# Spreading the idle groups of an edge loop between its blocks, and moving one small subtraction from ScalarE to VectorE

## The reference, cut to what matters

```
Wh    = xn @ W_w + W_b
e     = leaky(Wh[dst] . a_dst + Wh[src] . a_src + a_b, 0.2)
m     = segment_max(e, src)
ex    = exp(e - m[src])
att   = ex / segment_sum(ex, src)[src]
h     = relu(segment_sum(att * Wh[dst], src))
x     = x + h + mix(xn)
x     = x + ffn(layernorm(x))
```

## Time and profile before

| | us |
|---|---|
| three runs | 2430.62, 2435.78, 2439.38; median 2435.78 |
| the profiled execution | 2439.61, its span 2437.9 |
| first gather to last group's sums (in the edge loop) | 754.87 to 1914.06 |
| busy in the span: PE, DVE, ACT, POOL | 1952.8, 1758.0, 1440.8, 1129.3 |

### The profile page before, as it was taken

The page is one execution under the profiler, slowest core; times in us unless marked ns, Lnnn a source line. Parts: engine busy times, 40 slices in busy tenths (PEclk is TensorE's granted clock), DMA queues, the critical chain, the costliest instruction groups (busy, mean ns, idle before and its releaser), DMA issues. The chain is left out here.

```text
span 2437.9 us, 50376 instructions
## 1 busy us (share of the span) xinstructions
PE 1952.8 (80%) x10273; PEld 1581.1 (65%) x10273; DVE 1758.0 (72%) x5447; ACT 1440.8 (59%) x4447; POOL 1129.3 (46%) x1089
## 2 busy tenths in 40 slices
PE   2888856598874888988889998998799564399997
PEld 1444435477762777767677877777678463288886
DVE  7877769999984778787768888887788752155543
ACT  3566547233311778877778888887688762133332
POOL 0000000011125777777777777777720177455555
PEclk9899967799986999999999999999999875699998
DMA  4200000011112444444444444444410455255553
GB/s 136 59 26 27 28 2 22 13 55 23 24 21 76 121 118 116 122 124 117 121 117 118 121 117 121 117 116 121 124 41 6 123 141 139 75 88 92 94 97 57
DMA packets 123284, 205.68 MB, mean 84 GB/s; under 512 B 34806, under 2 KB 77667, under 8 KB 122987
## 3 DMA queue, kind: packets, MB, share of 16 engines
q0 software_dynamic: 69648, 135.12, 23.8%
q1 hardware_dynamic: 48681, 59.88, 8.3%
q10 hardware_dynamic: 4658, 7.46, 1.1%
HBM read 146.67 MB, written 49.70 MB: 81 GB/s over the span
## 5 line engine op out<-in xcount | busy, mean ns | idle before, releaser
L1306 POOL DMA_INDIRECT area<-wh_table,area x812 | 783.8, 965 | 260.1 <-issue 246.4
L1619 PE MATMUL bank<-area 128*126 x2008 | 512.4, 399 | 103.8 <-ACT area L1542 70.1
L1619 PEld LDWEIGHTS bank<-area 128*126 128x126 f32 x2008 | 366.6, 192 | 186.8 <-issue 134.0
L1340 DVE TENSOR_SCALAR area<-iota_row,area 128x126 f32<-128x126 f32 x1004 | 357.9, 364 | 33.1 <-ACT area L1495 27.5
L1528 ACT ACTIVATE area<-iota_row,area 128x126 f32<-128x126 f32 x753 | 292.4, 389 | 0.4 <-ACT area L1535 0.3
L1409 DVE SCALAR_TENSOR_TENSOR acc_mem<-acc_mem,area,bank 125x258 f32 x251 | 120.7, 481 | 179.6 <-PE bank L1607 168.1
L1542 ACT ACTIVATE area<-area 128x126 f32<-128x126 f32 x753 | 243.1, 387 | 0.5
L2110 POOL DMA_INDIRECT out_dram<-area x108 | 169.2, 1567 | 158.7 <-DVE area L2171 142.3
L519 POOL IOTA acc_mem<- 50x812 f32 x1 | 0.8, 807 | 457.7 <-DVE area L789 457.7
L1481 ACT ACTIVATE area<-bank 125x512 bf16<-125x512 f32 x251 | 148.7, 592 | 95.8 <-DVE area L1350 94.0
L1639 PE MATMUL bank<-area 128*128 128x250 f32 x800 | 191.0, 382 | 4.0 <-ACT area L1555 4.0
(11 more groups left out here) (395 smaller groups left out, 4217.1 us busy)
## 6 DMA issues: line engine op xcount, KB each, us to landing
area<-moe_rows SPq DMA_DIRECT2D x54, 264.0 KB, 2.7
area<-wh_table,area POOLq DMA_INDIRECT x812
area<-area SPq DMA_DIRECT2D x18, 388.5 KB, 3.4
wh_table<-area SPq DMA_DIRECT2D x50, 126.5 KB
xn<-in_x_dram SPq DMA_DIRECT2D x25, 250.0 KB
x_rows<-area SPq DMA_DIRECT2D x25, 250.0 KB
area<-x_rows ACTq DMA_DIRECT2D x24, 250.0 KB
area<-in_L_ffn_expert_w_dram SPq DMA_DIRECT2D x3, 1536.0 KB, 12.1
```

What stands on the lines that cost most here:

```text
L1306: g.indirect_dma_start(out=gath[:, (i + GT) % RS, :], out_offset=None, in_=table, in_offset=bass.IndirectOffsetOnAxis(ap=idx_tab[:, i:i + ...
L1340: ins = V.tensor_scalar(xm[:, b, t, :], iota_row[:, :], rowl[:, j % 10, t:t + 1], fetched(j, D)[:, t:t + 1], ALU.is_equal, ALU.mult)
L1619: last = T.matmul(bank[US[b]][0:RW, 0:WROW], sm[:, b, t, :], gath[:, bass.ds(place + t, 1), 0:WROW].rearrange("p a w -> p (a w)"), start=( ...
```

## The change

1. **Table.** The groups that no edge needs (`left` of them) are dealt out between the blocks: behind block i−1 there stand `int(i * left / 50 + 0.25)` of them in all. They carry block number 50, a 51st block of `acc`, `own_all`, `fr_c`, `peak` and `iota_blk` that nothing reads, and the first tile of the block that comes next. The table is worked out with a few more DVE instructions; two more small matmuls turn `tf` into a column for the ring's counts.
2. **Maximum.** `own_second` leaves ACT; `row_second` does the same subtraction on DVE, two slots behind the group's number, between `mark(2)` and `score_edge`. `d_m` now counts four steps to a group, and `a_own` one.
3. **Clearing.** The part of `acc_mem` from `ZERO_FROM` on (7798 of 13158 columns lie before it) is cleared ahead of the wait for the edge table; the rest is cleared in the loop, by a stage `clear` that runs once, at the end of slot 3, and `gather_up` of group 0 waits for it.

```
-        acc_mem = sb("acc_mem", [128, NT * WROW])
+        acc_mem = sb("acc_mem", [128, (NT + 1) * WROW])
+        acc_all = acc_mem[0:R, :].rearrange("p (b w) -> p b w", w=WROW)
...
+                V.tensor_tensor(packed[:, 3, :], firstf[:, 1:NT + 1], firstf[:, 0:NT], ALU.subtract)
                 step(V.tensor_tensor_scan(gend, ones[:, 0:NT], ngf, 0.0, ALU.mult, ALU.add))
...
+                step(V.tensor_scalar(left, gend[:, NT - 1:NT], -1.0, float(NG), ALU.mult, ALU.add))
+                V.tensor_copy(packed[:, 4, :], firstf[:, 1:NT + 1])
+                step(V.tensor_scalar(lastf, iota_g[:, 1:NT + 1], left, 1.0 / NT, ALU.mult, ALU.mult))
+                step(V.tensor_scalar(int50, lastf, 0.25, None, ALU.add))
+                step(V.tensor_copy(sparef[:, 1:NT + 1], int50))
+                V.tensor_tensor(packed[:, 0, :], gend, sparef[:, 1:NT + 1], ALU.add)
+                step(V.tensor_tensor(ngf, ngf, sparef[:, 1:NT + 1], ALU.add))
+                V.tensor_tensor(packed[:, 1, :], gend, sparef[:, 0:NT], ALU.add)
+                step(V.tensor_tensor(packed[:, 2, :], ngf, sparef[:, 0:NT], ALU.subtract))
+                step(V.tensor_tensor(packed, packed, ident[:, 0:NT].unsqueeze(1).to_broadcast([128, 6, NT]), ALU.mult))
+                step(V.tensor_reduce(cols, packed, AX.X, ALU.add))
...
+                step(V.tensor_copy(whole, ended))
+                V.tensor_tensor(shown, iota_g[0:1, :], groups, ALU.subtract)
+                step(V.tensor_tensor(spot, past, whole, ALU.subtract))
+                V.tensor_scalar(over, whole, -1.0, float(NT), ALU.mult, ALU.add)
+                step(V.scalar_tensor_tensor(shown, spot, -1.0, shown, ALU.add, ALU.mult))
+                V.tensor_tensor(over, spot, over, ALU.mult)
+                step(V.scalar_tensor_tensor(tf, shown, -float(GT), begun, ALU.mult, ALU.add))
+                V.tensor_tensor(over, over, whole, ALU.add)
+                V.tensor_scalar(tf, tf, float(TILES - GT), None, ALU.min).then_inc(gcmp_ready, 1)
+                dve.wait_ge(gcmp_ready, 2)
+                step(V.scalar_tensor_tensor(word, over, 65536.0, tf, ALU.mult, ALU.add))
...
+                V.memset(acc_mem[:, ZERO_FROM:], 0.0)
                 dve.wait_ge(tab_pe, 1)
...
+                pe.wait_ge(gcmp_ready, 2)
+                T.matmul(bank[KV][:, 508:509], tf[:, 0:L], ones[0:1, 0:1], start=True, stop=True)
+                T.matmul(bank[KV][0:NG - L, 509:510], tf[:, L:NG], ones[0:1, 0:1], start=True, stop=True).then_inc(gmap_done, 1)
...
-                V.memset(acc_mem[:, :], 0.0).then_inc(acc_zero, 1)
-                dve.wait_ge(acc_zero, 3)
+                dve.wait_ge(acc_zero, 2)
...
+                def clear(s, j):
+                    if at(s) == 0:
+                        V.memset(acc_mem[:, 0:ZERO_FROM], 0.0).then_inc(acc_zero, 1)
...
+                def row_second(s, j):
+                    n, r = at(s), block_of(j)
+                    dve.wait_ge(d_m, at(s, 4, 3))
+                    V.tensor_tensor(own_word(dve, r, n, 1), own_word(dve, r, n, 0), own_high(dve, r, n, 0), ALU.subtract).then_inc(d_m, 1)
...
+                    if at(s) == 0:
+                        dve.wait_ge(acc_zero, 3)
...
-                               (4, score_sum), (0, mark(2)), (4, score_edge), (0, mark(3)), (4, score_leaky), (5, own_weight),
-                               (4, score_less_max)], feed)
+                               (4, score_sum), (0, mark(2)), (2, row_second), (4, score_edge), (0, mark(3)), (4, score_leaky), (5, own_weight),
+                               (4, score_less_max), (3, clear)], feed)
...
-                def own_second(s, j):
-
-                    n, r = at(s), block_of(j)
-                    act.wait_ge(d_m, at(s, 3, 3))
-                    A.activation(own_word(act, r, n, 1), own_high(act, r, n, 0), ACT.Identity, bias=own_word(act, r, n, 0), scale=-1.0).then_inc(a_own, 1)
-
                 def own_third(s, j):
 
                     n, r = at(s), block_of(j)
-                    act.wait_ge(a_own, at(s, 2, 1))
+                    act.wait_ge(d_m, at(s, 4, 4))
...
-                together(act, roots, [(5, edge_exp), (3, own_second), (5, apart([0])), (2, spread), (3, own_third), (5, apart([1])), (3, rescale),
+                together(act, roots, [(5, edge_exp), (5, apart([0])), (2, spread), (3, own_third), (5, apart([1])), (3, rescale),
                                       (5, apart([2])), (-1, own_rows), (5, weigh)], feed)
...
-                    wait(pe, d_m, at(s, 3, -5))
+                    wait(pe, d_m, at(s, 4, -7))
...
-                    pe.wait_ge(a_own, at(s, 2, 2))
+                    pe.wait_ge(a_own, at(s, 1, 1))
```

More of the change, by code:

```diff
@@ L248, in gps_kernel @@
         iota_g, gcmp = take(NG), take(NG)[0:NT, :]
-        more = take(128)
         rstd_all, nmr = (take(NT)[0:R] for _ in range(2))
@@ L322, in gps_kernel @@
         int50, end50 = (a.bitcast(I32) for a in smallt[7:9])
-        firstf = take(NT + 1)
-        gcol, csrc, tcol, wcol, pcol, tq0, tq1 = (take(1) for _ in range(7))
+        firstf, sparef = take(NT + 1), take(NT + 1)
+        csrc, left, tq0, tq1 = (take(1) for _ in range(4))
+        cols = take(6)
+        gcol, rcol, scol, dcolf, tcol, pcol = (cols[:, i:i + 1] for i in range(6))
         srci, dsti = wpos.bitcast(I32), bpos.bitcast(I32)
@@ L335, in gps_kernel @@
         behind = take(L)[0:NT, :]
-        tf = take(NG)
+        tf = take(NG)[0:1, :]
         spot, whole, over = (take(NG)[0:1, :] for _ in range(3))
@@ L340, in gps_kernel @@
         rcmp = take(2, NB)
+        gspare = take(NG)[0:NT, :]
+        shown = take(NG)[0:1, :]
+        packed = take(6, NT)
+        ZERO_FROM = take.place[0]
         XB, QB, HEADS, NUM, DEN, OUT = 0, 1, 2, 3, 4, 5
@@ L801, in _ @@
                 V.memset(firstf[:, NT:NT + 1], float(TILES))
+                V.memset(sparef[:, 0:1], 0.0)
                 step(V.tensor_copy(ngf, int50))
+                V.tensor_tensor(packed[:, 3, :], firstf[:, 1:NT + 1], firstf[:, 0:NT], ALU.subtract)
                 step(V.tensor_tensor_scan(gend, ones[:, 0:NT], ngf, 0.0, ALU.mult, ALU.add))
-                step(V.scalar_tensor_tensor(ngf, ngf, -float(GT), firstf[:, 1:NT + 1], ALU.mult, ALU.add))
-                V.tensor_tensor(tmp50, tmp50, ident[:, 0:NT], ALU.mult)
@@ L806, in _ @@
[L806 to L812, removed]
@@ new lines, in _ @@
+                step(V.tensor_reduce(cols, packed, AX.X, ALU.add))
+                V.tensor_scalar(gspare, iota_g[0:NT, :], rcol[0:NT, :], None, ALU.is_ge)
+                V.tensor_scalar(gcmp, iota_g[0:NT, :], gcol[0:NT, :], None, ALU.is_ge).then_inc(gcmp_ready, 1)
+                V.memset(own_all[:, NT:NT + 1, 0, :], 0.0)
+                V.memset(fr_c[:, NT:NT + 1], 0.0)
+                step(V.tensor_scalar(own_all[:, 0:NT, 0, 0], frd, csrc[0:R, :], None, ALU.add))
+                step(V.tensor_tensor(own_all[:, 0:NT, 0, 1], own_all[:, 0:NT, 0, 0], own_bits[:, 0:NT, 0, 0], ALU.subtract))
@@ L820, in _ @@
+                V.tensor_tensor(own_all[:, 0:NT, 0, 2], own_all[:, 0:NT, 0, 1], own_bits[:, 0:NT, 0, 1], ALU.subtract)
+                V.tensor_scalar(fr_c[:, 0:NT], own_all[:, 0:NT, 0, 0], shift[0:R, :], None, ALU.subtract)
                 attend(NT + 7)
                 dve.wait_ge(gmap_done, 1)
-                step(V.scalar_tensor_tensor(tf, iota_g, float(GT), bank[KV][:, 128:128 + NG], ALU.mult, ALU.add))
-                V.tensor_scalar(over, bank[KV + 1][0:1, 128:128 + NG], float(NT - 1), None, ALU.min)
@@ L829, in _ @@
[L829 to L833, removed]
@@ L834, in _ @@
-                step(V.tensor_scalar(spot, tf[0:1, :], float(GT), None, ALU.add))
+                begun, ended = bank[KV][0:1, 0:NG], bank[KV + 1][0:1, 0:NG]
+                groups, past = bank[KV][0:1, 256:256 + NG], bank[KV + 1][0:1, 256:256 + NG]
+                step(V.tensor_copy(whole, ended))
+                V.tensor_tensor(shown, iota_g[0:1, :], groups, ALU.subtract)
+                step(V.tensor_tensor(spot, past, whole, ALU.subtract))
+                V.tensor_scalar(over, whole, -1.0, float(NT), ALU.mult, ALU.add)
@@ L835, in _ @@
+                step(V.tensor_scalar(spot, tf, float(GT), None, ALU.add))
                 step(V.tensor_scalar(turns, spot, 0.5, 1.0 / RS, ALU.add, ALU.mult))
@@ L970, in _ @@
                 act.wait_ge(prefilled, 16)
-                A.activation(Sv[:, 0, :], iota_blk[:, :], ACT.Copy, scale=0.0)
+                A.activation(Sv[:, 0, :], iota_blk[:, 0:NT], ACT.Copy, scale=0.0)
                 for i in range(3):
@@ L1233, in gps_kernel @@
         pair = take(GT, 2)
-        peak = take(NT)
+        peak = take(NT + 1)
         e1, e2, e3 = (take(2, GT) for _ in range(3))
@@ L1322, in block_of @@
                 def block_of(j):
-                    return dve.snap(blocks[j % 10], min_val=0, max_val=NT - 1)
+                    return dve.snap(blocks[j % 10], min_val=0, max_val=NT)
```

57 lines of the change are left out of this document (26 added, 31 removed).

## The result

| | before | changed |
|---|---|---|
| median of the runs | 2436.77 us | 2394.68 us |
| ratio, 95% interval | | 0.983 [0.98, 0.986] |
| profiled execution (its span) | 2439.61 (2437.9) | 2389.63 (2387.9) |
| start to first gather | 754.87 | 752.31 |
| first gather to last sums | 1159.19 | 1109.37 |

The changed kernel is faster by 42 us, where 79 had been forecast, and its 2394.68 us lie 4.7 us above the end of the range, 2390. The whole gain lies in the edge loop (−49.8 us in the profiled execution). I read the changed kernel's slices and costliest groups first.

A forecast was written before the change was run, and what follows sets the result against it. Gathers on POOL bound the loop to 1786 us, then 25 edgeless groups ran alone. Loop 82 us off, table 3 on: 2439.6 − 79 = 2360.6 profiled, 2357 as median against 2435.8; range 2340 to 2390.

The forecast's parts named there:

- The two limits: Edge loop: 812 gathers at 1.270 us make 1031 us, 251 groups at 4.13 us make 1037; before, partly added.
- where the groups go: Edge loop: the 25 groups without edges, 103.8 us at the end, run between blocks in time the gathers need anyway.
- the walk: Stepping 203 gather batches and 251 groups through four timing rules; at pace 4.15 the last group starts at 1808 to 1812 us.
- The signs named for it: Last gather near 1800 us, last `own_rows` within 10; many times the room waits; fewer `ready` waits; `gather_up` 4.1 to 4.2.
- The second word: `row_second` on DVE instead of ACT: +0.05 us a group, between −0.08 and +0.17; pace taken as 4.15 us.
- ACT's relief: Edge loop: the instruction taken from ACT saves at most 0.285 us; −0.2 each in slots 6 and 7.
- Clearing and table: Clearing ahead of and in the loop costs nothing lasting; the table's longer DVE chains add 3 us, between 1.5 and 5.
- Rival 1: Edge loop: DVE becomes the bound, pace 4.30, 45 us off in all, 2391 us; chance 0.14.
- The sum's own upper end: Second word's slot sum at its highest: +0.17 us a group, with 0.28 in six slots and nothing won.
- Rival 2: Edge loop: ACT's relief outweighs DVE's load and gathers bind; pace 4.05, about 2346 us; chance 0.17.
- Rival 3: Edge loop: gathers stand still behind the new DVE instruction, 40 us over 812 gathers, 2382 us; chance 0.04.
- Rivals 4 and 5: Edge loop: 4, dealing out brings nothing, within 0.3% (0.03); 5, slower, ACT, DVE and PE no longer overlap, 2464 (0.05).

The follow-up runs named there:

- The dummy with `row_second`'s operands: Changed kernel with the second word back on ACT, plus a DVE subtraction reading `row_second`'s operands behind the same wait, result unread: 2388.86 us, ratio 0.9809.

## Why the prediction was wrong

**The two limits, and where the groups go:** right. With its own pace put in, the walk gives the last `own_rows` at 1844, which is 1089 us behind the first gather; measured are 1086.1. At 4.13 it gives 1050 to 1054, and the kernels with the second word on ACT took 1047.5 both times. So the walk is 3 to 7 us long, and the overlap worth a little more than it says. The signs named for it are there: room waits 23 times those of before, eight waits of `own_rows` for `ready` (61 before). The last gather came not at 1800 but at 1826, because the groups held it up.

**The second word: this is the step that failed.** The prediction put row_second at "from nothing ... to 0.28 us; I take 0.2", and ACT's relief at −0.2 in slots 6 and 7, for +0.05 us a group. By the medians of `gather_up`'s period in each slot (second word on ACT, then changed):

| slot | 0 | 1 | 2 | 3 | 4 | 5 | 6 | 7 | 8 | 9 | sum |
|---|---|---|---|---|---|---|---|---|---|---|---|
| on ACT | 3.75 | 3.75 | 4.48 | 3.97 | 4.17 | 4.11 | 4.16 | 4.28 | 4.06 | 4.13 | 40.86 |
| changed | 4.12 | 4.12 | 4.84 | 4.33 | 4.31 | 4.13 | 4.05 | 4.39 | 4.06 | 4.14 | 42.49 |
| measured | +0.37 | +0.37 | +0.36 | +0.36 | +0.14 | +0.02 | −0.11 | +0.11 | 0 | +0.01 | +1.63 |
| predicted | +0.2 | +0.2 | 0 to +0.1 | +0.2 | +0.2 | 0 | −0.2 | −0.2 | 0 | 0 | +0.5 |

Which slots are DVE's was read nearly right: 0 to 3 wholly, where slot 2 had been given at most 0.1, and 4 in part. Two sizes were off. Slots 0 to 4 took 1.60 us more in place of 0.9, and slots 5 to 9 0.03 more in place of 0.4 less; together that is the 1.13 us that the ten slots are longer than predicted. The price is 0.37 us, above even the upper bound: that bound took its size from `row_leaky`, for which the trace lists one FUSED_REGOPS and an ALU_OP of 0.045 us, and behind which `score_sum` follows at once, needing no step. `row_second` needs two FUSED_REGOPS, and each of the two instructions behind it needs one of its own. And ACT's relief is worth nothing: −0.11 and +0.11 in the two slots where it was to bring −0.4. The dummy with `row_second`'s operands shows the same: ACT keeps its 0.285 us there, and the time is 2388.86, not above the changed kernel's 2392.67. DVE's slack says what was left over. Lines from 1000 to 1700 us, `gather_up` in the changed kernel:

```profile
L1441 DVE SCALAR_TENSOR_TENSOR acc_mem<-acc_mem,area,bank 125x258 f32 x163 | 78.0, 478 | 33.5 <-PE bank L1633 27.4 <-issue 5.2
```

and with the second word on ACT:

```profile
L1437 DVE SCALAR_TENSOR_TENSOR acc_mem<-acc_mem,area,bank 125x258 f32 x169 | 81.1, 480 | 70.9 <-PE bank L1635 63.5 <-issue 6.9
```

0.42 us of idle time a group fell to 0.21, so 0.21 of the 0.37 went into waits that were there, and 0.16 into the pace. Over 251 groups that is 41 us, against 38 between the two kernels on one chip.

**Clearing and table.** The clearing is free in either place, as said. The table's chain is 3.8 us longer where it stands, inside the 1.5 to 5 given, but nothing of it arrives. The shift of `int50` and the first sorting instruction behind the chain, then the last of the sort; kernel before, then changed:

```profile
466.79 0.18 DVE L800 TENSOR_SCALAR acc_mem<-acc_mem 128x50 int32<-128x50 int32 x1
...
479.91 1.63 DVE L853 TENSOR_TENSOR area<-acc_mem 128x2968 f16<-128x2968 f16 x1
...
732.85 0.22 DVE L868 SCALAR_TENSOR_TENSOR area<-area,bank 106x64 f32<-106x64 f32 x1 [3.81 <-ACT area L1047]
```
```profile
463.86 0.18 DVE L806 TENSOR_SCALAR acc_mem<-acc_mem 128x50 int32<-128x50 int32 x1
...
480.75 1.63 DVE L871 TENSOR_TENSOR area<-acc_mem 128x2968 f16<-128x2968 f16 x1
...
729.99 0.22 DVE L886 SCALAR_TENSOR_TENSOR area<-area,bank 106x64 f32<-106x64 f32 x1 [3.81 <-ACT area L1066]
```

13.12 us became 16.89, but the end of the sort lies 266.06 and 266.13 us behind the same instruction. The waits of DVE for PE in between took it up; they fell from 10.0 to 7.0 us. "Hardly any idle time" was read off the chain itself and not off the 250 us behind it. That error was 3 us the other way.

**The rivals.** Rival 1 is what happened, in its pace (4.30), nearly in its time (2391, where 2394.68 was measured) and in its sign (`gather_up`'s waits halved, though not gone). Its chance of 0.14 was too small, and the range was cut through its middle. The sum's own upper end, +0.17 us a group, had been its pace. Rival 2 is refuted by the relief being worth nothing. Rival 3: the gathers' median spacing, from the timeline, is 1.25 us in the changed kernel and 1.26 before; 60 spacings are over 1.35 us, of which 18 are waits for room and bring nearly all of the delay; the other 42 are short, and there were 37 of them before. So the rule of the Trainium skill's "SBUF — State Buffer" ("Who interferes with whom") costs nothing that these runs show. By the same section of the Trainium skill `tensor_tensor` had not been seen to stall a DMA; these runs agree, and the prediction left it out. Rivals 4 and 5 didn't occur.

## What to carry to other kernels

Before a small instruction is moved to an engine with short instructions, look at what its sequencer must do for it and for the instructions behind it: with two steps of register arithmetic it cost 0.37 us of DVE here, or 0.21 where the followers had no step, with one short step 0.10, with fixed addresses 0.05. Price it from `mark` to `mark`, start to start, not by its own length and the idle time ahead of it. And when a change takes away the wait that made engines idle, as laying the groups between the blocks did, each tenth of a microsecond in a group begins to count 251 times: make the two parts of such a change apart, since the one brought 80 to 87 us and the other took 38 of them back.

## What was unexpected of the hardware

- An instruction of 0.16 us delays the engine by 0.37 us at one place and 0.21 at the next, with all of the engine's records at their usual length and no idle time shown; only the sequencer's records tell the places apart.
- A wait of DVE for its own step three instructions back costs nothing: 2357.32 with it, 2355.83 without.
- On one chip the kernel before took 2801.26 us, 15% more than on the others. In the trace of the second word on ACT from that chip nearly all of the excess lies in the edge loop (1533.7 us from first gather to last sums, where it is 1069.9 elsewhere), with `gather_up` still for up to 8.7 us at a time. The cause is open.
